# Layer 0: how often TensorE is given attention over the values

## The reference

```python
qkv = jnp.einsum('btd,ed->bte', x, w_in) + b_in
q, k, v = jnp.split(qkv, 3, axis=-1)          # then (B, H, T, hd)
scores = jnp.einsum('bhqd,bhkd->bhqk', q, k) * scale
scores = jnp.where(allowed, scores, -1e30)     # |i - j| <= 128
attn = jax.nn.softmax(scores, axis=-1)
ctx = jnp.einsum('bhqk,bhkd->bhqd', attn, v)
out = jnp.einsum('btd,ed->bte', ctx, w_out) + b_out
return x + out
```

## Time and profile before

| | |
|---|---|
| median of 3 runs | 660.29 us (657.98 to 662.27) |
| the profiled execution's own time | 659.7 us |
| its span | 657.9 us |
| attention units of layer 0 | from about 53 to 351 us of the span |
| a full batch in the steady part | 38.6 to 39.0 us |
| layer 1 | from about 360 us to the end |

### The profile page before, as it was taken

One profiled execution on the slowest core, in us unless ns is written; L12 is line 12 of the kernel. 1 busy time (PEld: TensorE's weight loads), 2 busy tenths in 40 slices (PEclk: granted clock), 3 DMA queues, 4 the chain that ended last, 5 costly groups with the idle time before them and its releaser, 6 DMA issues. The chain is left out here.

```text
span 657.9 us, 18248 instructions
## 1 busy us (share of the span) xinstructions
PE 539.2 (82%) x5803; PEld 315.1 (48%) x5804; DVE 449.9 (68%) x1874; ACT 358.6 (55%) x1069; POOL 307.0 (47%) x350
## 2 busy tenths in 40 slices
PE   5399999898998989899995898888635999999920
PEld 4134444444444444444443576556332666666610
DVE  7597898887878879788912698888751454545416
ACT  4404777777776776776773565666402444444410
POOL 6653736355461635610000378888740555555520
PEclk9655999999999999999997699999876999999965
DMA  3836181644627155370102511211111222222209
GB/s 96 175 101 125 51 178 36 156 101 119 131 64 163 55 143 103 95 150 4 35 27 74 212 50 51 68 56 56 57 53 33 70 74 75 73 73 75 72 19 368
DMA packets 51142, 61.14 MB, mean 93 GB/s; under 512 B 9969, under 2 KB 41973, under 8 KB 49280
## 3 DMA queue, kind: packets, MB, share of 16 engines
q1 hardware_dynamic: 45568, 49.67, 30.5%
q0 software_dynamic: 4352, 8.47, 3.8%
q10 hardware_dynamic: 1152, 2.10, 0.8%
HBM read 32.01 MB, written 28.45 MB: 92 GB/s over the span
## 5 line engine op out<-in xcount | busy, mean ns | idle before, releaser
L639 DVE CUSTOM_DVE_ANT_0 A<-A,band 128x320 f32<-128x320 f32 (+2 forms) x512 | 214.0, 463 | 47.6 <-PE A L801 46.6
L502 ACT ACTIVATE Pb<-SB 128x320 f32<-128x320 f32 (+2 forms) x512 | 175.4, 402 | 86.5 <-PE SB L837 84.4
L801 PE MATMUL A<-Ks,Qs 48*64 48x320 bf16 (+2 forms) x1024 | 131.9, 310 | 10.6 <-DVE mneg L639 4.4
L828 PE MATMUL SB<-Qs,Ks 50*64 50x320 bf16 (+2 forms) x1024 | 126.7, 294 | 12.6 <-ACT Pb L502 10.8
L828 PEld LDWEIGHTS SB<-Qs,Ks 50*64 50x64 bf16 x1024 | 55.9, 106 | 102.8 <-ACT Pb L502 85.7
L1603 POOL DMA_INDIRECT results<-y,xt x72 | 70.7, 982 | 71.3 <-issue 37.0
L837 PE MATMUL SB<-ends,ident 64*64 64x64 bf16 (+1 forms) x1024 | 98.1, 206 | 0.0
L850 PE MATMUL PV<-Pb,Va 128*32 128x320 f32 (+2 forms) x1024 | 86.4, 410 | 0.4 <-ACT Pb L502 0.4
L1707 PE MATMUL UP<-w_up,xT 128*128 x144 | 80.1, 639 | 1.6 <-ACT xT L1616 1.2
L1649 DVE COPY hT<-HT 128x256 f32<-128x256 f32 x72 | 30.5, 424 | 63.2 <-PE HT L1678 63.2
L1165 POOL DMA_INDIRECT expert_rows<-pay,pos x64 | 62.9, 982 | 22.9 <-issue 17.5
(11 more groups left out here) (225 smaller groups left out, 937.5 us busy)
## 6 DMA issues: line engine op xcount, KB each, us to landing
Qs<-parts_dram SPq DMA_DIRECT2D x16, 384.0 KB, 5.9
Ks<-parts_dram SPq DMA_DIRECT2D x16, 384.0 KB, 9.4
xt<-expert_rows SPq DMA_DIRECT2D x72, 65.0 KB, 1.8
yb<-results SPq DMA_DIRECT2D x8, 512.0 KB, 6.7
parts_dram<-qp SPq DMA_DIRECT2D x16, 192.0 KB, 2.9
parts_dram<-kp SPq DMA_DIRECT2D x16, 192.0 KB, 2.8
l_xb<-x_dram SPq DMA_DIRECT2D x9, 256.0 KB, 2.7
xb<-in_x SPq DMA_DIRECT2D x8, 256.0 KB, 2.9
```

Of the source, the lines that this page charges most:

```text
L502: act.activation(Pb[:, group % 4, c, 0:w], SB[k % NB_BANKS][:, 0:w], ACT.Exp).then_inc(act_exp, 1)
L639: nc.vector.tensor_tensor_reduce(scores_of, scores_of, band[:, skip:skip + w], -1.0, 3e38, ALU.add, ALU.min, mneg[:, step % 2, col:col + 1 ...
L801: mm = nc.tensor.matmul(A[k % NA_BANKS][out:out + HP, 0:w], Qs[b % RING][rows, a, HP * sub:HP * sub + HP], Ks[b % RING][rows, a, lo:lo + w ...
L828: nc.tensor.matmul(out[r0:r0 + HP, 0:w], Ks[b % RING][rows, a, HP * sub:HP * sub + HP], Qs[b % RING][rows, a, lo:lo + w], start=True, stop ...
```

## The change

`attend` no longer runs once every four units but for two groups one behind the other every eight: at `u` = 2, 10, 18, 26, 34, 42, 50 and 58 for groups (-2, -1), (0, 1), (2, 3), (4, 5), (6, 7), (8, 9), (10, 11) and (12, 13). Odd groups stay at the `u` where they were (group 1 at 10, 3 at 18 and so on). Even groups move from 14, 22, 30, 46, 54 and 62 to four units later, and groups 0 and 8 from 7 and 39 to 10 and 42. The batch's last two groups are at `u` = 2 of the next batch, and behind the loop for the last one. The products themselves, their number and their order are the same. No other engine's program is edited.

```diff
@@ -937,11 +937,12 @@
                         turn_xq(g, (dve_x1, b) if b > 0 else (act_k1, g))
                     if u == 56:
                         ffn_mm(g, (act_mT, STEPS * b + 3))
-                if u % UNITS == 7 or u % HG == 2 and u % UNITS != 6:
-                    group = NS * (STEPS * b) + u // HG - 1
-                    if group >= 0:
-                        attend(group // NS, group % NS)
-        attend(NSTEP - 1, NS - 1)
+                if u % (2 * HG) == 2:
+                    for group in range(NS * (STEPS * b) + u // HG - 2, NS * (STEPS * b) + u // HG):
+                        if group >= 0:
+                            attend(group // NS, group % NS)
+        for sub in (NS - 2, NS - 1):
+            attend(NSTEP - 1, sub)
         turn_ctx(NB - 1, 0, misc, (dve_x1, NB - 1))
         turn_ctx(NB - 1, 1, A[0], (dve_max, UNITS * NSTEP))
         turn_ctxn(NB - 1, (dve_ctx, 2 * NB))
```

## The result

The changed kernel takes 674.47 us (median of 4 runs, 672.7 to 675.2) against 659.87 us for the kernel before in the same session: ratio 1.0214, 95% interval 1.0193 to 1.0235. It is 14.6 us slower. The prediction was 669, with 653 to 678 as its range.

A forecast was written before the change was run, and what follows sets the result against it. No single engine was taken as the bound; plain stretches were bounded by TensorE's absence against three banks of stock. Place terms of +1.35 us a full batch summed to +8.8 on 659.7, predicting 669 us, range 653 to 678.

The forecast's parts named there:

- The second group pays streaming alone: In each pair, the second attend costs only its columns' streaming, 0.32 to 0.53 us, without the fixed part.
- pair (0, 1): At u = 10: turn_ctx follows one unit later and VectorE is out of stock; +0.3 us a full batch.
- (2, 3): Pair at u = 18: VectorE has contexts beside its maxima and doesn't idle; +0.1 us, between 0 and +0.2.
- (4, 5): Pair at u = 26: pushes the chain of q projection, evacuations and k projection; +0.5 us.
- (6, 7): Pair at u = 34: VectorE idle before its next piece, ScalarE has evacuations of k queued; +0.3 us.
- (8, 9): Pair at u = 42: removing the attend at 39 gives back 0.47, 0.32 is paid; -0.15 us.
- (10, 11): Pair at u = 50: removing the attend at 46 gives back 0.68, 0.53 is paid; -0.15 us.
- the last two: Pair (12, 13) in the plain stretch, +0.05 us, and pair (14, 15) at u = 2 before values, +0.4 us.
- The granted clock is 1.00 in these windows, so it plays no part: In the profiled windows of the kernel before, TensorE's clock is 1.00; the forecast has no term for it.
- a second group that pays its fixed part again: In every pair, 0.14 us more per second group, 9 us on top: 678 us, counted as the forecast's far end.
- rival that idle time only moves: Across batches, undisturbed units offset longer absences; a batch grows about +0.2 us, in all 1 to 2: 662 us; chance 0.32.
- rival that the drains decide: TensorE's own time is the path; each pair saves 0.26 us: 643.7 us, or 652 in half the places; chance 0.18.

The follow-up runs named there:

- cut run: Kernel before with groups 4 and 5 at u = 26, score matmuls at u = 20 to 25 doubled, group 4 cut to 64 columns: 658.79 us, ratio 0.9985.
- shifted run: Kernel before with groups 1 and 2 at u = 14, 3 and 4 at 22, 5 and 6 at 30, nothing at 10, 18, 26: ratio 1.0102.
- run with one pair: Kernel before with only groups 4 and 5 paired at u = 26, nothing at 22: 669.41 us, ratio 1.016.
- two runs with filling in it: Kernel before, groups 4 and 5 at u = 26, score matmuls at u = 20 to 25 doubled; uncut 1.0056, group 4 cut to 64 columns 0.9985.

## Why the prediction was right, and what it missed

*That it gets slower, and by which mechanism: right.* TensorE's time in attention over the values fell by 11.6 us, and VectorE's and ScalarE's waits for TensorE rose by 15 to 16. Its busy time as a whole did not fall by the forecast's "some 10 us": 540.8 for 539.2. The groups of lines 801, 828 and 837 (pieces and scores) grew by 2.3, 4.7 and 2.0 us; in a batch without a fall TensorE is busy 34.49 us for 34.94. Matmuls at the lower clock are part of this, and the rest stays open. The forecast was +8.8 us, measured is +14.6.

*The second group pays streaming alone: right.* 1.28 against 0.74 us at 320, 0.96 for 192 with 256; one for one with columns in the cut run. What a pair saves is 2 x 0.74 - 1.28 = 0.20 us, for the forecast's 0.26.

*The terms of a batch: right in sign at every place of a full batch, near in size.* Forecast and measured in batch 2: pair (0, 1) +0.3 and +0.32; (2, 3) +0.1 and +0.22; (4, 5) +0.5 and +0.54; (6, 7) +0.3 and +0.34; (8, 9) -0.15 and -0.13; (10, 11) -0.15 and -0.14; the last two +0.45 and +0.47. The sum of a batch is 1.61 for 1.35. Batch 6 with the start of 7 grew by some 1.5 where 0.8 was forecast. The term that was wrong there is the pair (10, 11): the -0.15 rested on TensorE's wait at 46, batch 6 has none, and the pair costs 0.54. The end gave back about 0.5, as the wait of the earlier trace rows promised. In all, placement was 11.2 us (counted from `u` = 25 of batch 0) for 8.8.

*Why removals gave nothing at 7, 14, 22, 30 and 62: right, and more general than I put it.* I named evacuations and contexts beside which they lay. The shifted run shows that the kept places at 10 and 26 are of the same kind: one attend just fills a wait. My statement there, that the pair pushes the chain, was right; I would have been wrong, and in the shifted run was, to conclude that taking the attend away pulls the chain forward.

*"The granted clock is 1.00 in these windows, so it plays no part": wrong.* This is the step that failed, and it is the term missing from the sum. The clock was 1.00 with an attend every four units, and I took it as given for a schedule that has none for eight. It is 5.7 us of the profile's 14.8. In the run with one pair both falls follow the stretch from which an attend was taken, and cost 1.5 us each there; in the two runs with filling in it there is none. Against a simple rule stand two falls behind a standstill of TensorE of 1.7 to 2.1 us that no moved attend explains. Which stretches are hit isn't settled: with work put into one stretch, falls came behind others, and single profiles can't say how they vary from run to run.

*That 674.5 lies within the range is partly luck.* The room above 669 was kept for a second group that pays its fixed part again, and that did not happen; the missing clock filled it. And the near fit of what is left, 14.8 - 5.7 = 9.1 for 8.8, comes of placement forecast 2.4 too low and of 2.1 us given back that I had not forecast: the clock's earlier rise (1.0) and layer 1 (1.1).

*The rival that idle time only moves* is out: the chains at 26, 34 and 2 had no slack (+0.54, +0.34 and +0.47), and a batch grew by 1.61 us where that rival wanted about 0.2.

*The rival that the drains decide* is out: it needs TensorE to wait for no bank between attends. It holds at two places (42 and 50), at -0.13 and -0.14 us each. The rule cited from the Trainium skill, "TensorEngine Tiling (Array Packing)", section Tiling Modes, that changing the tiling mode drains TensorE, agrees with the shorter pairs (1.28 against 2 x 0.74), though no run here parts a drain from other fixed costs of a visit; it says nothing of who waits.

## What to carry to other kernels

When work on a well used engine is moved together to save its fixed costs, ask at each place who waits for the longer absence. A step that exactly fills a wait costs nothing singly and in full when doubled, so the sum goes place by place, from the timeline, and not from busy shares. And work that seems to be in nobody's way may be part of what keeps TensorE's clock up: before thinning out a stretch, count the clock among its rows.

## What the runs showed of the hardware

- Two float32 attends in a row on the same 32-column tiles run on without a gap: 16 matmuls take 1.28 us where 8 take 0.74. The fixed part is about 0.2 us a visit, not a matmul.
- A fall of the granted clock to 0.50 lasts 3.4 us at a time here. It made a pair of 0.96 us take 1.72, one of 1.28 take 2.36, and each cost the schedule 1.2 to 1.5 us.
- Issuing a bank's score matmuls twice isn't free where TensorE seems to wait: with 32 of the 64 units doubled, batches were about 0.8 us longer (41.2 for 40.35).
- TensorE can stand still for 1.66 and 2.09 us in one profile and not in another of nearly the same kernel (`u` = 13 of batch 1); a fall of the clock followed both times, within 0.2 us of its next matmul. The trace names nothing that it waited for.
